# A second message stage that gathers each edge tile's source rows once, into a ring of 64 slots

## The reference, cut to what matters

```python
# x: 6250 nodes x 256; src, dst: 106250 edges, sorted by dst; f32 throughout
def layer0(h, ei, ej, d2):            # first message stage
    msg = silu(concat(h[ei], h[ej], d2) @ mW1 + mb1)
    msg = silu((layer_norm(msg) * ln_g + ln_b) @ mW2 + mb2)
    agg = segment_sum(msg, ei, 6250)
    return h + silu(concat(h, agg) @ uW1 + ub1) @ uW2 + ub2
def layer1(x, src, dst):              # second message stage
    agg = segment_sum(x[src], dst, 6250)
    cnt = segment_sum(ones, dst, 6250)
    return relu((agg / max(cnt, 1)) @ W.T + b)
x = layernorm(x + layer0(x, src, dst, edge_weight1))
x = layernorm(x + layer1(x, src, dst))
```

## Time and profile before

| | us |
|---|---|
| median of three runs | 4849.86 (4846.39 to 4852.14) |
| span of the profiled execution, first to last instruction | 4536.7 |
| that execution's own time | not printed; the median stands 313.2 above the span |
| first gather of the second message stage | at 3264.13 |
| last addition of that stage | begins at 4402.58 |
| busy over the span: PE, PEld, DVE, ACT, POOL | 3096.1, 2307.5, 2802.5, 1601.4, 3137.6 |

### The profile page before, as it was taken

The page is one execution under the profiler, slowest core; times in us unless marked ns, Lnnn a source line. Parts: engine busy times, 40 slices in busy tenths (PEclk is TensorE's granted clock), DMA queues, the critical chain, the costliest instruction groups (busy, mean ns, idle before and its releaser), DMA issues.

```text
span 4536.7 us, 80206 instructions
## 1 busy us (share of the span) xinstructions
PE 3096.1 (68%) x16582; PEld 2307.5 (51%) x16583; DVE 2802.5 (62%) x13616; ACT 1601.4 (35%) x2993; POOL 3137.6 (69%) x2714
## 2 busy tenths in 40 slices
PE   5877777777777777777777777759555555555554
PEld 2365555555555555555555555548433333333332
DVE  4476666666666666666666666647655555555557
ACT  0355555555555555555555555533100000000001
POOL 0068888888888888888888888861177777777750
PEclk9999999999999999999999999989777777777778
DMA  8345555555555555555555555575433333333333
GB/s 286 107 72 83 83 84 83 83 83 84 83 83 83 83 83 83 83 83 84 83 84 83 83 83 83 83 135 160 125 103 102 103 102 103 104 102 103 102 92 104
DMA packets 314015, 444.07 MB, mean 98 GB/s; under 512 B 50464, under 2 KB 257404, under 8 KB 313724
## 3 DMA queue, kind: packets, MB, share of 16 engines
q0 software_dynamic: 211200, 346.20, 41.0%
q1 hardware_dynamic: 102524, 95.40, 7.1%
HBM read 280.15 MB, written 161.01 MB: 97 GB/s over the span
## 4 chain that ended last, share of the span: by engine, by line
POOL 29%; issue 23%; DMA 20%; PE 13%; ACT 5%; DVE 4%; SPq 4%; DVEq 1%; POOLq 0%; ACTq 0%
POOL sum L464 15%; POOL work L451 14%; DMA work<-x_tab,idx 13%; PE ps L710 9%; DMA work<-p_tab,idx 6%; ACT work L814 2%; PE ps L670 2%; ACT work L799 2%; DVE work L1090 2%; ACT work L778 1%; SPq L329 1%; PE ps L688 1%; SPq L349 1%; SPq L343 1%; DMA sum<-work,sidx 1%
## 5 line engine op out<-in xcount | busy, mean ns | idle before, releaser
L464 POOL DMA_INDIRECT sum<-work,sidx x880 | 1400.9, 1592 | 291.2 <-issue 236.2
L451 POOL DMA_INDIRECT work<-p_tab,idx x880 | 864.0, 982 | 489.1 <-issue 267.1
L451 POOL DMA_INDIRECT work<-x_tab,idx x880 | 840.5, 955 | 344.0 <-issue 159.1
L710 PE MATMUL ps<-work 128*125 128x257 f32 x1760 | 646.0, 531 | 527.8 <-DMA work<-x_tab,idx 516.6
L628 PE MATMUL ps<-w,work 128*128 128x256 f32 x3520 | 888.6, 385 | 151.4 <-ACT work L814 151.3
L710 PEld LDWEIGHTS ps<-work 128*125 128x125 f32 x1760 | 437.6, 261 | 735.9 <-issue 464.3
L628 PEld LDWEIGHTS ps<-w,work 128*128 128x128 f32 x3520 | 601.5, 191 | 306.8 <-issue 183.7
L1090 DVE TENSOR_TENSOR work<-ps,work 128x512 f32<-128x512 f32 x440 | 283.4, 686 | 664.1 <-DMA work<-p_tab,idx 650.0
L1291 DVE TENSOR_TENSOR big<-ps,big 125x257 f32 x880 | 375.6, 427 | 380.1 <-PE ps L710 332.6
L616 PE MATMUL ps<-big,work 128*128 x2640 | 371.6, 283 | 334.1 <-DVE work L1090 333.2
L778 ACT ACTIVATE work<-work 128x512 f32<-128x512 f32 x440 | 274.2, 623 | 759.3 <-DVE work L1090 759.3
(11 more groups left out here) (167 smaller groups left out, 4356.8 us busy)
## 6 DMA issues: line engine op xcount, KB each, us to landing
sum<-zeros SPq DMA_DIRECT2D x4, 6400.0 KB
work<-sum SPq DMA_DIRECT2D x200, 128.0 KB, 2.2
work<-p_tab,idx POOLq DMA_INDIRECT x880
sum<-work,sidx POOLq DMA_INDIRECT x880
work<-x_tab,idx POOLq DMA_INDIRECT x880
work<-x_tab SPq DMA_DIRECT2D x50, 128.0 KB, 2.1
pxin<-in_x_dram SPq DMA_DIRECT2D x50, 112.0 KB
p_tab<-prow SPq DMA_DIRECT2D x50, 112.0 KB
```

The source lines that it names most:

```text
L451: pool.indirect_dma_start(out=slots[:, par, u, 0:D], out_offset=None, in_=table[:, :], in_offset=bass.IndirectOffsetOnAxis(ap=idx[:, par, ...
L464: pool.indirect_dma_start(out=sums[u][:, :], in_=tot[:, par, u, :], in_offset=None, out_offset=bass.IndirectOffsetOnAxis(ap=sidx[:, par, u ...
L710: nc.tensor.matmul(ps[0:NB, u, 0:CW], same[:, par, u, 0:NB], msg[:, par, u, 0:CW], start=True, stop=True).then_inc(e[1]["agg"], 1)
```

## The change

The second message stage gathers by tile, not by visit: 832 gathers (208 quads of tiles, the last one padding), each with a semaphore wait on a constant, written out one after the other on POOL. They write a ring of 64 row slots, tile t into slot t modulo 64. PE finds the slot of a visit in a register, loaded for each quad from a new table `vslot`, which DVE works out in the preparation as (v - block) modulo 64. The indices of the gathers come from a new table `esrc`, made by seven transposes of `ends` on PE and a DVE copy. The DVE copies of `vsrc` into `idx` go from this stage, with their waits. From tile 15 on, gather t waits until visit t-15 has been multiplied. PE waits, for visit quad q below 208, for the gathers of tile quad q; for quads 208 to 219 it waits for no gather. `big` and `work` become parts of one area `arena`; ring and one-hots lie in it behind `rows`.

```diff
+TILE_QUADS = -(-TILES // QT)
+RING = 64
+BEHIND = BLOCKS - 1
...
+        arena = sb("arena", [P, BIG_W + WORK_W])
+        big = arena[:, 0:BIG_W].bitcast(bf16).rearrange("p (j k d) -> p j k d", j=BLOCKS, k=PARTS)
+        rows = arena[:, 0:ROWS_W].rearrange("p (j c) -> p j c", j=BLOCKS)
+        ring = arena[:, ROWS_W:ROWS_W + RING * CW].rearrange("p (s c) -> p s c", s=RING)
+        same1 = arena[:, SAME1:SAME1 + 2 * QT * NB].rearrange("p (a u n) -> p a u n", a=2, u=QT)
...
+        vslot = sb("vslot", [P, VISITS], i32)
+        esrc = sb("esrc", [P, CHUNKS * P], i32)
...
-            steps(pool, QUADS, 0, gather(1, x1_tab, msg), by=4)
+            pool.wait_ge(s_esrc, 1)
+            for tile in range(TILE_QUADS * QT):
+                if tile >= RING - BEHIND:
+                    pool.wait_ge(e[1]["agg"], tile - (RING - BEHIND) + 1)
+                pool.indirect_dma_start(
+                    out=ring[:, tile % RING, 0:D], out_offset=None, in_=x1_tab[:, :],
+                    in_offset=bass.IndirectOffsetOnAxis(ap=esrc[:, tile:tile + 1], axis=0))\
+                    .then_inc(s_ring[tile // QT % 4], 16)
...
             pe.wait_ge(s_visit, 4)
+            for c in range(CHUNKS):
+                last = nc.tensor.transpose(ps[:, PP + c // 4, c % 4 * P:(c % 4 + 1) * P], ends[:, 0, c, :], ident[:, :])
+            last.then_inc(s_esrct, 1)
...
+            def aggregate(q, k_):
+                par = k_ % 2
+                pe.load(slot_regs, vslot[0:1, bass.ds(q * QT, QT)])
+                at = [pe.snap(reg, min_val=0, max_val=RING - 1) for reg in slot_regs]
                 pe.wait_ge(e[1]["hot"], q + 1)
-                pe.wait_ge(e[1][f"gat{par}"], half_count(q) * (16 * QT))
+                if not isinstance(q, int) or q < TILE_QUADS:
+                    pe.wait_ge(s_ring[k_], (q // 4 + 1) * (16 * QT))
                 for u in range(QT):
                     if later(q, 1):
                         pe.wait_ge(e[1]["acc"], (q - 1) * QT + u + 1)
-                    nc.tensor.matmul(ps[0:NB, u, 0:CW], same[:, par, u, 0:NB], msg[:, par, u, 0:CW],
+                    nc.tensor.matmul(ps[0:NB, u, 0:CW], same1[:, par, u, :],
+                                     ring[:, bass.ds(at[u], 1), :].rearrange("p a c -> p (a c)"),
                                      start=True, stop=True).then_inc(e[1]["agg"], 1)
+            pe.wait_ge(s_slots, 5)
             pe.wait_ge(s_ones, 1)
-            steps(pe, QUADS, 0, aggregate, by=4)
+            for q in range(4):
+                aggregate(q, q)
+            with pe.Fori(1, TILE_QUADS // 4) as it:
+                for k_ in range(4):
+                    aggregate(it * 4 + k_, k_)
+            for q in range(TILE_QUADS // 4 * 4, QUADS):
+                aggregate(q, q % 4)
...
+            nc.vector.tensor_tensor(viota[:, :], viota[:, :], vdst[:, :], ALU.subtract).then_inc(s_slots, 1)
...
+            nc.vector.scalar_tensor_tensor(out=vslot[:, :], in0=wrest[:, 0, :], scalar=float(-RING), in1=viota[:, :],
+                                           op0=ALU.mult, op1=ALU.add).then_inc(s_slots, 1)
...
+            nc.vector.tensor_copy(esrc[:, :], flat(ps[:, PP:PP + 2, :])[:, 0:CHUNKS * P]).then_inc(s_esrc, 1)
...
-            nc.vector.memset(msg[:, :, :, D:CW], 1.0).then_inc(s_ones, 1)
+            nc.vector.memset(ring[:, :, D:CW], 1.0).then_inc(s_ones, 1)
...
             def step_1(q, par):
                 if live(q + 1, QUADS):
                     one_hot_1(q + 1, 1 - par)
-                if live(q + 2, QUADS):
-                    stage(q + 2, par, 1)
                 if isinstance(q, int) and q == 0:
                     clear_rows()
                 if live(q, QUADS):
                     accumulate(q, par)
-            steps(dve, QUADS, 0, step_1, ahead=2, by=4)
+            steps(dve, QUADS, 0, step_1, ahead=1, by=4)
```

More of the change, by code:

```diff
@@ L103, in gnn @@
         cnt = sb("cnt", [NB, 2, BLOCKS])
-        work = sb("work", [P, 12544])
+        work = arena[:, BIG_W:BIG_W + WORK_W]
         at_ = [0]
@@ L231, in gnn @@
         s_xrows, s_x1st, s_out, s_ones = sem("s_xrows"), sem("s_x1st"), sem("s_out"), sem("s_ones")
+        s_slots, s_esrct, s_esrc = sem("s_slots"), sem("s_esrct"), sem("s_esrc")
+        s_ring = [sem(f"s_ring{i}") for i in range(4)]
         EDGE = [["staged", "gat0", "gat1", "hot", "hott", "hev", "keyt", "apart", "same", "dup", "dif", "sidx", "qexp", "pre",
                  "keys", "placed", "silu", "bst", "mom", "newt", "norm", "ztr", "zev", "mm", "msg", "ded", "tot", "added"],
-                ["staged", "gat0", "gat1", "hot", "agg", "acc"]]
+                ["hot", "agg", "acc"]]
         e = [{n: sem(f"e{l}_{n}") for n in EDGE[l]} for l in range(2)]
@@ L439, in _, with gather_0 @@
                 pool.wait_ge(s_pst[par], 32 * BLOCKS // 2)
[L441 to L455, removed]
+            def gather_0(q, par):
+                pool.wait_ge(e[0]["staged"], q + 1)
+                if later(q, 2):
+                    pool.wait_ge(e[0]["pre"], 2 * (q - 1))
+                pool.sem_inc(s_turn_pool, 1)
+                for u in range(QT):
+                    pool.indirect_dma_start(
+                        out=gat[:, par, u, 0:D], out_offset=None, in_=p_tab[:, :],
+                        in_offset=bass.IndirectOffsetOnAxis(ap=idx[:, par, u:u + 1], axis=0))\
+                        .then_inc(e[0][f"gat{par}"], 16)
             def add(q, par):
@@ L467, in add @@
                         compute_op=ALU.add).then_inc(e[0]["added"], 16)
-            gather_0 = gather(0, p_tab, gat)
             def step_0(q, par):
@@ L701, in _ @@
             steps(pe, BLOCKS, 4, block_0, by=4)
-            def aggregate(q, par):
+            slot_regs = [pe.alloc_register(f"pe_slot{u}") for u in range(QT)]
+            def aggregate(q, k_):
+                par = k_ % 2
+                pe.load(slot_regs, vslot[0:1, bass.ds(q * QT, QT)])
+                at = [pe.snap(reg, min_val=0, max_val=RING - 1) for reg in slot_regs]
                 pe.wait_ge(e[1]["hot"], q + 1)
-                pe.wait_ge(e[1][f"gat{par}"], half_count(q) * (16 * QT))
+                if not isinstance(q, int) or q < TILE_QUADS:
+                    pe.wait_ge(s_ring[k_], (q // 4 + 1) * (16 * QT))
                 for u in range(QT):
@@ L1172, in beside @@
                         if i == 2:
-                            stage(q + 2, par, 0)
+                            stage(q + 2, par)
                             nc.vector.tensor_copy(loc[:, par, :], vloc[:, bass.ds((q + 2) * QT, QT)])\
@@ L1277, in one_hot_1 @@
                 for u in range(QT):
-                    last = nc.vector.tensor_scalar(same[:, par, u, 0:NB], nodes[:, :], vloc[:, bass.ds(q * QT + u, 1)],
+                    last = nc.vector.tensor_scalar(same1[:, par, u, :], nodes[:, :], vloc[:, bass.ds(q * QT + u, 1)],
                                                    None, ALU.is_equal)
```

32 lines of the change are left out of this document (24 added, 8 removed).

## The result

| | before | changed | ratio (95%) |
|---|---|---|---|
| whole time, us, 4 runs each | 4848.12 (4841.85 to 4852.14) | 4720.78 (4713.41 to 4726.9) | 0.9742 (0.973 to 0.9754) |
| profiled execution: span / own time | 4536.7 / not printed | 4715.4 / 4717.16 | |

The change takes 127 us off, against 31 predicted, and the time lies 98 us under the forecast and 80 us under its range. Yet the span of the new profile is 179 us *longer* than that of the old one. The new page says why a first doubt is due: a span of 4715.4 and a time of 4717.16 leave 1.8 us outside the span, where I had left 313.

What follows compares the result with a forecast made beforehand. POOL's issue of gathers was taken as the bound of the second stage. Fewer gathers (-60.5), the stop (-9.9) and the last 12 quads (+39.6) sum to -30.8 us, from 4849.86 to 4819 us, range 4801 to 4840.

Steps and rivals of the forecast that it cites:

- 313.2 us above the span: Whole kernel: the median measured time's excess over the profiled span, carried over unchanged into the forecast.
- POOL's issue of gathers is the bound: Second message stage: gathers issued 1.26 us apart set the pace, while PE and DVE wait.
- 48 gathers at 1.26: Second stage, POOL: 832 gathers instead of 880 remove 48 steps of 1.260 us, -60.5 us.
- stop at the start: Second stage: POOL's single 10.18 us standstill at the thirteenth gather goes, -9.9 us.
- seven long steps: Second stage, POOL: steps of 3.3 us instead of 1.26, 112 gathers apart; forecast to stay.
- rival A: Second stage: the seven long steps vanish with POOL's loop, a further -14.3 us, giving 4805 us; chance 0.14.
- 12 quads after the last gather: Second stage end: visit quads 208 to 219, no longer hidden behind gathers, cost 3.3 us each, +39.6 us.
- outside the stage: Preparation and the rest: slot numbers and tile indices are hidden in idle time, 0, at most +5 us.
- D: Second stage start: the stop stays because the memset still holds the first additions; -20.9 us, 4829 us; chance within forecast's 0.62.
- Rival B: Second stage: new code stalls POOL, up to +21 us, or last quads take 4.4 us; 4825 to 4853; chance 0.15.
- Rival C: Second stage: PE becomes the bound, its quad cycle above 5.04 us; at 5.4, +56 us, 4906; chance 0.07.

Runs made afterwards that it cites:

- e1: The kernel before, unchanged, profiled once more in a session with spells: 4857.3 us, ratio 1.0009, span 4840.5 us.
- e18: The changed kernel, unchanged, run again in a session without spells: 4504.25 us, ratio 0.9918 to the kernel before.
- e13: The changed kernel, unchanged, run again in another session without spells: 4504.56 us, ratio 0.9915 to the kernel before.
- e4: The changed kernel with every 17th gather doubled into a spare tile, 880 in all; without spells: 4561.84 us, ratio 1.0053 to the kernel before.
- e3: The changed kernel with gather t waiting for visit t-8 instead of t-15; without spells: 4502.46 us, ratio 0.9917 to the kernel before.
- e16: The changed kernel with 880 gathers, DVE's index copy, POOL waiting for that copy, and room 8; without spells: 4565.81 us, ratio 1.0048 to the kernel before.
- e2: The kernel before with the second stage's 880 gathers written out on POOL; with spells: 4819.33 us, ratio 0.9928 to the kernel before.
- e9: The changed kernel with DVE's copy of four indices per quad kept, POOL not waiting for it; with spells: 4744.95 us, ratio 0.987 to the kernel before.
- e10: The changed kernel with DVE's index copy kept, POOL waiting for it before each four gathers, and room 8; with spells: 4705.44 us, ratio 0.9793.
- e11: The changed kernel with the second stage's one-hots built on ACT instead of DVE; with spells: 4654.03 us, ratio 0.9683 to the kernel before.

## Why the prediction was wrong, by its own steps

**The step that failed** is in its sum: "The median of the three runs, 4849.86, stands 313.2 us above the span, and I leave that part as it is". Whole times lie 1.8 us above their span. The gap was a sign that the profiled execution and the timed ones did not run alike, and it was carried over as a constant. In e1 it lies within the span, 291.6 us of it in the second stage. With that, "POOL's issue of gathers is the bound; PE and DVE wait for it" was true of the profiled execution and not of the timed ones: in e1 POOL's mean step is 1.619 us, not 1.26, and POOL stands idle for DVE's copy (183.1 us) and for PE (172.4).

**The mechanism held where the kernel ran as profiled.** e18 against the profile of before, one trace each, by the terms:

| | predicted | measured |
|---|---|---|
| 48 gathers at 1.26 | -60.5 | -84.2 for the three, first to last gather (1131.6 to 1047.4) |
| stop at the start | -9.9 | |
| seven long steps | kept; -14.3 in rival A | |
| 12 quads after the last gather | +39.6 | +41.4 (6.8 to 48.2), 3.39 a quad |
| outside the stage | 0, at most +5 | +8.4 (+5.0 ahead of it, +3.4 after), scatter included |
| sum | -30.8 | -34.4 (spans: 4502.2 - 4536.7 = -34.5) |

-60.5 - 9.9 - 14.3 is -84.7, so rival A is right: no step of e13 or e18 over 1.5 us is left, and their gathers are written out. e4, with 880 written-out gathers, has none either, so it isn't the count of gathers that brings them. The median gain, 36 to 38 us, lies between forecast and rival A; the stop's end (against D) and the 3.3 us of the last quads were right. For the stop the prediction gave both reasons, the room and the earlier memset, and against D it named only the room; e3 gives the memset 9.0 of the 9.9 us. The term outside the stage was put at 0 and measured +8.4, above its bound, but no price can be read from two traces: in the ten traces of ring kernels without spells the first gather starts between 3265.2 and 3269.4. Rival B, a stall by new code, showed nothing: between 3400 and 4300 of e18 five instruction packets came, with no gap in POOL's steps. Here the trace agrees with the Trainium skill (Runtime: NRT & Kernel Launch, Instruction fetch mechanics), that straight-line fetching is mostly hidden; that the branch was what cost the 2 us is not shown, since the loop's form was only removed, not varied. Rival C (PE as the bound) didn't come in this form. A check on the account is e16: with 48 gathers and the coupling put back, only the 12 uncovered quads, the missing stop and long steps, and the +8.4 outside remain, 39.6 - 9.9 - 14.3 + 8.4 = +23.8, or +25.6 with the 41.4 measured for the quads; e16 measured +22.9. The agreement is good to a few us, no more, as the +8.4 is uncertain.

**With spells the same change is worth 127 us**, and most of the difference is found, though not its division among the parts. I cut the two traces (e1 and the changed kernel, of two sessions) into quads of additions and sorted them by whether a sequencer instruction of DVE of 0.6 us or more starts in them:

| | quads hit | us | quads free | us |
|---|---|---|---|---|
| before (e1) | 127 | 1021.3 (8.04 each) | 93 | 387.7 (median 3.85) |
| changed | 104 | 883.0 (8.49 each) | 116 | 400.6 (median 3.39) |

Together the quads take 125.4 us less. The columns can't be subtracted one by one, as 23 quads moved from the first to the second. By the means (8.04 and 4.17 before, 8.49 and 3.45 changed): 23 quads that are free and no longer hit, at 3.87, bring 89; 116 free quads that are 0.72 shorter bring 83; 104 hit quads that are 0.45 longer take 47 back. The first addition comes 14.0 us after the first gather in place of 21.1, which makes up the rest of the 132.6. The free ones cost 3.39 to 3.85 us, less than the 5.04 that four gathers take, since their rows were gathered during the spell before; so I read neither kind of quad as bound by POOL's issue: the free ones go at the cycle of PE and DVE, the hit ones at that of DVE's sequencer. The sums of DVE's sequencer time point the same way: spells add 296.1 us to it before and 274.9 after (535.3 against 260.4 in e18), and 291.6 and 201.9 us to the stage. A rival is PE's granted clock, which in this stage is 0.61 in e1 and 0.68 in the changed kernel where the profile of before has 0.76. It can't be the main part: a quad's matmuls take 3.79 us at the low clock and a hit quad 8.0 to 8.5, and of the additions' 600.0 us of idleness only 104.3 are for PE. The written-out form is worth 31 to 38 us (e2).

**What stays open.** How the other 89 to 96 us divide between the 48 gathers, DVE's copy with its wait and the earlier memset: e9, with the copy kept, gains 60 us beside a kernel before of 4805 us, where the changed kernel itself was not run, and e10 contradicts a simple price for the copy. And what the spells are. They begin about 8 us after POOL has started on gathers back to back (medians 7.8 us in the changed kernel and 7.9 in e1, some seven gathers) and end 2 to 3 us after it pauses (medians); they don't occur in the first message stage, where additions stand among the gathers; the sessions that have them also show PE's granted clock at 0.89 to 0.90 in the first message stage, where the others have 0.99. That gathers on POOL bring them on is thus argued from their times; no run had this stage without gathers.

## What to carry to other kernels

Before a sum is made, hold the profiled execution's span against the measured time: here 1.8 us is the normal distance, and 313 us meant that the profile was of another condition than the times, under which a different engine set the pace. Look in such a case at the minimum and maximum of sequencer instructions, not at busy time or medians: DVE's agreed throughout. And price a change in both conditions: moving DVE's one-hots to ACT gave 0.9898 without spells and 0.9683 with them, the lowest time of its session in either, while the copy on DVE was free in the one and not clearly so in the other.

## What the runs showed of the hardware

- DVE's sequencer can fall into spells in which one instruction after another takes 0.70 us: register operations of 0.057, an ALU operation of 0.045, a register load of 0.34; its data instructions keep their 426 ns. It occurs only in the stage whose gathers go back to back and only in some sessions; 64 spells of 9.6 us in 1.3 ms. Nearly always it is DVE (456 instructions in the changed kernel); with the one-hots on ACT (e11) PE's sequencer had 30 beside DVE's 249, and ACT's none.
- POOL's 2-us pauses every 112 gathers of a loop are gone in the written-out form, with 832 gathers and with 880.
- The register load took 332 or 333 ns on PE and 342 to 344 on DVE in every trace (medians). On DVE its longest was 378 in the traces without spells, and 724 in the changed kernel and 1395 in e1. On PE one load of slot numbers, the first, took 1028 in the changed kernel and 1632 in e18.
